# LeakyReLU on ScalarE out of PSUM, the mask from tanh in one pass, banks of their own, and a new order of all stages

## The reference

```
out  = conv3x3(x2, conv1) + b1
out  = (out - mean) * rsqrt(var + eps)          # per image and channel
out  = where(out >= 0, out, 0.2 * out)
out1 = conv3x3(out, conv2) + b2
mask = sigmoid(conv3x3(out, mask_w) + mask_b)
xm   = out * mask
q, k, v = 1x1 convolutions of xm (k and v of the padded xm)
attn = softmax over the 3x3 neighbours of sum_c q * k
out2 = sum over the neighbours of attn * v
y    = x2 + out1 * mask + (1 - mask) * out2
```

## Time and profile before

| | |
|---|---|
| median of 3 runs | 208.28 us (207.56 to 209.03) |
| the profiled execution | 207.95 us |
| its span, first to last instruction | 206.2 us |
| busy: PE, PEld | 177.2 us (86%), 117.6 us (57%) |
| busy: DVE, ACT, POOL | 153.4 us (74%), 106.3 us (52%), 71.2 us (35%) |
| granted TensorE clock, mean | 0.992 |

### The profile page before, as it was taken

The page is one execution under the profiler, slowest core; times in us unless marked ns, Lnnn a source line. Parts: engine busy times, 40 slices in busy tenths (PEclk is TensorE's granted clock), DMA queues, the critical chain, the costliest instruction groups (busy, mean ns, idle before and its releaser), DMA issues.

```text
span 206.2 us, 7265 instructions
## 1 busy us (share of the span) xinstructions
PE 177.2 (86%) x3161; PEld 117.6 (57%) x3161; DVE 153.4 (74%) x362; ACT 106.3 (52%) x192; POOL 71.2 (35%) x60
## 2 busy tenths in 40 slices
PE   1699989999867999999687999999688798999981
PEld 1557727748454555787347456876446344666841
DVE  6796499948697968697788993993838765992782
ACT  2173554313683732718982714449614774955650
POOL 8600530550005411750008640850404022670390
PEclk9999999999999999999999999999999789999999
DMA  6512014000230000001000040000100000000002
GB/s 190 104 57 60 0 26 121 10 10 6 76 103 29 0 15 10 3 6 41 0 3 0 0 122 5 6 3 13 56 3 5 0 3 10 5 8 5 6 0 105
DMA packets 11312, 6.34 MB, mean 31 GB/s; under 512 B 9168, under 2 KB 9648, under 8 KB 11280
## 3 DMA queue, kind: packets, MB, share of 16 engines
q1 hardware_dynamic: 11040, 5.29, 9.9%
q10 hardware_dynamic: 240, 0.58, 0.9%
HBM read 3.35 MB, written 1.05 MB: 21 GB/s over the span
## 4 chain that ended last, share of the span: by engine, by line
PE 56%; DVE 18%; ACT 9%; issue 6%; DMA 4%; SPq 3%; POOL 1%; DVEq 0%; ACTq 0%
PE ps L1473 9%; PE ps L1376 8%; PE ps L1435 7%; PE ps L1349 5%; PE ps L1342 5%; PE ps L1386 4%; PE ps L1536 3%; DVE sh_in L326 3%; DMA w3b<-in_w_gi 3%; PE ps L1508 2%; PE ps L1497 2%; SPq L395 2%; PE ps L1334 2%; PE ps L1519 2%; ACT p_t L733 2%
## 5 line engine op out<-in xcount | busy, mean ns | idle before, releaser
L483 POOL TENSOR_TENSOR ln_s<-ln_s,neg_half 128x16 f32<-128x16 f32 x7 | 20.5, 2929 | 63.3 <-DVE ln_s L940 63.3
L1435 PE MATMUL ps<-ln_out,w_gi 32*64 32x256 f32 x1152 | 33.7, 377 | 1.2 <-DVE x L1082 0.8
L1435 PEld LDWEIGHTS ps<-ln_out,w_gi 32*64 32x64 f32 x1152 | 25.6, 130 | 7.3 <-issue 2.4
L1376 PE MATMUL ps<-w_qk,sh_ln 128*128 128x128 f32 x192 | 23.2, 278 | 3.6 <-DMA sh_ln<-ln_out 2.4
L1473 PE MATMUL ps<-sh_in,w_in 96*32 96x256 f32 x384 | 23.8, 396 | 1.5 <-DVE sh_in L326 1.5
L1376 PEld LDWEIGHTS ps<-w_qk,sh_ln 128*128 128x128 f32 x192 | 22.1, 192 | 5.1 <-issue 4.0
L1342 PE MATMUL ps<-busy 128*128 128x512 bf16 x79 | 21.3, 407 | 0.0
L1473 PEld LDWEIGHTS ps<-sh_in,w_in 96*32 96x32 f32 x384 | 11.9, 114 | 12.5 <-issue 3.6
L618 ACT ACTIVATE sh_ln<-ln_out 32x512 f32<-32x512 f32 (+1 forms) x29 | 15.2, 524 | 5.2 <-DVE ln_out L918 4.8
L618 ACT ACTIVATE sh_x<-x 32x496 f32<-32x496 f32 (+1 forms) x20 | 12.3, 616 | 3.7 <-DVE x L1082 3.2
L618 ACT ACTIVATE sh_in<-act_c 32x496 f32<-32x496 f32 (+1 forms) x20 | 12.3, 617 | 3.2 <-DVE act_c L1140 2.9
(11 more groups left out here) (142 smaller groups left out, 333.1 us busy)
## 6 DMA issues: line engine op xcount, KB each, us to landing
x_res<-in_x SPq DMA_DIRECT2D x4, 256.0 KB, 2.9
out_x<-out_s SPq DMA_DIRECT2D x4, 256.0 KB, 2.5
sh_ln<-ln_out SPq DMA_DIRECT2D x15, 64.0 KB, 2.1
x_norm<-in_x SPq DMA_DIRECT2D x3, 256.0 KB, 3.0
kc<-in_shape_consts ACTq DMA_DIRECT2D x1, 450.0 KB, 5.0
w3b<-in_w_gi SPq DMA_DIRECT2D x1, 288.0 KB, 5.2
x_norm<-in_x SPq DMA_DIRECT2D x2, 128.0 KB, 2.8
ln_out<-ln_out SPq DMA_DIRECT2D x8, 25.5 KB, 2.4
```

What stands on the lines that cost most here:

```text
L483: nc.gpsimd.tensor_tensor(ln_s[n][:, 3, :], ln_s[n][:, 2, :], neg_half[:, :], ALU.pow)\
L1376: mm = nc.tensor.matmul(to, sh_ln1[pair % 2][:, d, i, WD * y:WD * y + P], w_qk[:, dy, :, :, :].rearrange("p d m c -> p (d m c)"), start=(d ...
L1435: mm = nc.tensor.matmul(ps[EC * i:EC * i + EC, r, BLK * m:BLK * m + BLK], w_gi[rows, dx, m, dy, :], src[rows, i, dy:dy + RH, dx:dx + W], s ...
```

## The change

- ScalarE computes LeakyReLU (Prelu, alpha 0.2) straight from conv1's PSUM bank, two images one after the other, with the negated mean (plus the conv's bias) as bias; `conv1_evac`, `center` and VectorE's `lrelu` go. One more small VectorE operation makes that bias, `I_NEG`.
- `scaled_act` also halves, and `masked` is (th + 1) * act_in, per image; msk goes. 1 - msk is made by VectorE from th, behind `masked`. The halo and `window_q` wait for `masked` alone.
- Of the planes "in", the block s = 1, r = 0 goes to DMA on SP, ScalarE's s = 1 block to VectorE; VectorE still has seven. The planes ln1 of pair 3 are shared out as those of pair 2.
- Head scores, attention output and r1 get banks of their own; `qk` then waits for the gated product of the pair in front, not for x2. The x1 sum is a stage of its own.
- The order of the stages on all engines is new. Six gate rounds stand behind `window_q` and `window_k`, where fillers stood; half of image 1's qk comes before conv1; on VectorE `ln1_apply` of pair 3 stands before the window probabilities. Fillers: 17 in the head's front become 6, and 9 in each step go.
- Banks 4 and 7 are cleared at the start by VectorE; POOL's constant of ones goes.

The diff, cut, first the signals and banks:

```diff
+        planes_by["in"]["dma"] = signal("in_planes_dma", 16, start=1)
         def head_bank(pair):
-            return 6 if pair == 1 else 3
+            return (3, 5, 7, 7)[pair]
+        def attn_bank(pair):
+            return (3, 5, 4, 4)[pair]
+        def reduce_banks(pair):
+            return (0, 1) if pair == PAIRS - 1 else (6, 7)
```

On SP's queue:

```diff
+            def in_planes(pair):
+                sp.wait_ge(g_lr.sem, g_lr.done(pair))
+                sp.wait_ge(g_c2.sem, g_c2.before(pair))
+                sp.dma_start(plane(sh_in)[C:2 * C, :, 1:1 + RH, :],
+                             act_c[0:C, :, :].rearrange("p i (y x) -> p i y x", x=W))\
+                  .then_inc(planes_by["in"]["dma"].sem, 16)
             def step(pair, norm):
-                if norm:
-                    load_norm(pair + 3)
                 load_res(pair + 2)
+                in_planes(pair)
                 ln2_edges(pair + 1)
                 halo(pair)
...
+            load_norm(2)
             ln1_planes(1)
-            load_norm(2)
             load_res(1)
+            load_norm(3)
```

On POOL:

```diff
             def step(pair, norm):
-                complement(pair)
-                residual(pair)
                 if norm:
                     rstd(0, pair + 3)
+                    residual(pair)
                     rstd(1, pair + 2)
...
```

On ScalarE:

```diff
-            def conv1_evac(pair, early=False):
...
+            def lrelu(pair, early=False):
+                act.wait_ge(g_in.sem, g_in.at(pair, 5))
+                act.wait_ge(g_sc.sem, g_sc.before(pair))
+                for e in ("dve", "dma"):
+                    act.wait_ge(planes_by["in"][e].sem, planes_by["in"][e].before(pair))
+                for i in range(2):
+                    ins = nc.scalar.activation(act_c[:, i, :], ps[:, conv1_bank(early), BLK * i:BLK * i + BLK], ACT.Prelu,
+                                               bias=inorm_v[:, I_NEG, i:i + 1], alpha=SLOPE)
+                ins.then_inc(g_lr.sem, 1)
             def step(pair, norm):
                 load_exp_table()
+                qk_t_evac(pair + 2, 0)
                 squares(1, pair + 1)
-                conv1_evac(pair)
-                qk_t_evac(pair + 2, 0)
+                lrelu(pair)
                 qk_t_evac(pair + 2, 1)
...
+                x2_planes(pair + 1)
                 pv_evac(pair)
-                x2_planes(pair + 1)
...
             key_windows(last)
             probs_t(but_last)
+            window_exp(last)
             out1_evac(last, True)
-            window_exp(last)
```

On VectorE:

```diff
+            for bank in (4, 7):
+                nc.vector.memset(ps[:, bank, :], 0.0).then_inc(s_zero_bd, 1)
...
             def masked(pair):
                 dve.wait_ge(g_th.sem, g_th.done(pair))
-                nc.vector.tensor_scalar(msk[:, :], th[:, :], 0.5, 0.5, ALU.mult, ALU.add).then_inc(g_xm.sem, 1)
...
+                for i in range(2):
+                    ins = nc.vector.scalar_tensor_tensor(
+                        out=xm[:, i, 1:1 + RH, 1:1 + W],
+                        in0=th[:, BLK * i:BLK * i + BLK].rearrange("p (y x) -> p y x", x=W), scalar=1.0,
+                        in1=act_in[:, i, :].rearrange("p (y x) -> p y x", x=W), op0=ALU.add, op1=ALU.mult)
+                ins.then_inc(g_xm.sem, 1)
+            def complement(pair):
...
+                nc.vector.tensor_scalar(omm[pair % 2][:, :], th[:, :], -0.5, 0.5, ALU.mult, ALU.add).then_inc(g_xm.sem, 1)
             def step(pair, norm):
+                if norm:
+                    x1_sum(pair + 1)
                 ln2_center(pair + 1)
+                inorm(pair)
                 ln_var(1, pair + 1)
-                inorm(pair)
                 inorm_mean(pair)
-                center(pair)
                 variance(pair)
-                lrelu(pair)
                 in_planes(pair)
+                ln2_apply(pair + 1)
                 head_scores(pair + 2)
-                ln2_apply(pair + 1)
                 scaled_act(pair)
                 head_max(pair + 2)
                 masked(pair)
+                complement(pair)
                 head_mix(pair + 2)
                 if norm:
                     ln1_center(pair + 3)
+                x1_sum(pair + 2)
+                if norm:
+                    ln_var(0, pair + 3)
                 else:
                     ln2_center(pair + 2)
                 window_softmax(pair)
-                ln_var(*((0, pair + 3) if norm else (1, pair + 2)))
-                window_probs(pair)
                 if norm:
                     ln1_apply(pair + 3)
                 else:
+                    ln_var(1, pair + 2)
+                window_probs(pair)
+                if not norm:
                     ln2_apply(pair + 2)
                 gated(pair + 1)
                 x2_all(pair + 1)
...
             ln1_center(2)
-            dve.wait_ge(s_wgi, 3)
-            clear(ps[:, 4, :], ps[:, 7, :])
+            ln_var(0, 2)
             ln2_apply(0)
             head_scores(1)
-            ln_var(0, 2)
+            ln1_apply(2)
             head_max(1)
             head_mix(1)
```

On TensorE:

```diff
             def qk(pair, i, halves=(0, 1)):
...
-                if not is_first(pair):
-                    pe.wait_ge(g_x2.sem, g_x2.before(pair - 1))
+                if pair > 1:
+                    pe.wait_ge(g_gi.sem, g_gi.at(pair - 2, 1))
             def step(pair, norm):
-                if not is_first(pair):
-                    attn_out(pair + 1)
                 qk(pair + 2, 0)
+                qk(pair + 2, 1, (0,))
                 conv1(pair)
+                qk(pair + 2, 1, (1,))
                 average_mean(pair)
-                qk(pair + 2, 1, (0,))
+                v_by_head(pair + 2, (0,))
                 average_var(pair)
-                qk(pair + 2, 1, (1,))
+                v_by_head(pair + 2, (1, 2))
                 gram(pair + 2)
-                v_by_head(pair + 2)
-                mask_conv(pair)
+                mask_conv(pair, images=(0,))
                 by_head(pair + 2)
+                mask_conv(pair, images=(1,))
+                front_read(pair + 2)
                 conv2(pair)
-                front_read(pair + 2)
-                stay_busy(2 if norm else 5, 5)
                 window_q(pair)
-                window_k(pair, busy_for=4)
-                if norm:
-                    stay_busy(3, 2)
-                else:
-                    attn_out(pair + 2)
+                gate_info(pair + 1, range(3))
+                window_k(pair)
+                gate_info(pair + 1, range(3, 6))
+                pe.wait_ge(g_q_sb.sem, g_q_sb.done(pair))
+                attn_out(pair + 2)
                 window_scores(pair)
+                pe.wait_ge(g_x1.sem, g_x1.done(pair + 2))
                 window_v(pair)
-                pe.wait_ge(g_x1.sem, g_x1.done(pair + 1 if norm else pair + 2))
-                gate_info(pair + 1, range(12))
+                gate_info(pair + 1, range(6, 15))
                 probs_transposed(pair)
-                gate_info(pair + 1, range(12, 18))
+                gate_info(pair + 1, range(15, 18))
                 window_out(pair)
...
             pe.wait_ge(s_busy, 1)
-            stay_busy(12, 5)
-            pe.wait_ge(g_im[0].sem, g_im[0].done(0))
-            stay_busy(5, 5)
+            stay_busy(4, 5)
             pe.wait_ge(s_wready, W_QKV)
             qk(0, 0)
+            stay_busy(2, 5)
             qk(0, 1)
...
-            pe.wait_ge(g_x2.sem, g_x2.done(but_last))
+            pe.wait_ge(g_gi.sem, g_gi.done(but_last))
             gate_info(last, range(6))
```

More of the change, by code:

```diff
@@ L206, in build @@
                      "dma": [(0, 2), (0, 3), (1, 0), (1, 1)]}
-        copies[2] = {"dve": [(3, r) for r in range(R)], "act": [(2, r) for r in range(R)],
-                     "dma": [(s, r) for s in (0, 1) for r in range(R)]}
+        for n in (2, 3):
+            copies[n] = {"dve": [(3, r) for r in range(R)], "act": [(2, r) for r in range(R)],
+                         "dma": [(s, r) for s in (0, 1) for r in range(R)]}
         g_xn = signal("x_for_norm_loaded", 16)
@@ L457, in _ @@
             but_last, last = PAIRS - 2, PAIRS - 1
+            in_planes(but_last)
             halo(but_last)
+            in_planes(last)
             halo(last)
@@ L591, in _ @@
             residual(but_last)
-            complement(last)
             residual(last)
@@ L762, in step @@
                 q_evac(pair)
+                if norm:
+                    squares(0, pair + 3)
                 k_evac(pair)
@@ L816, in _ @@
             out1_evac(but_last)
-            conv1_evac(last, True)
             q_evac(but_last)
+            lrelu(last, True)
             k_evac(but_last)
@@ L1112, in inorm_mean @@
                 dve.wait_ge(g.sem, g.at(pair, 4))
+                nc.vector.scalar_tensor_tensor(out=inorm_v[:, I_NEG, :], in0=inorm_v[:, I_MEAN, :], scalar=-1.0,
+                                               in1=vec[:, V_BC1:V_BC1 + 1].broadcast_to([P, 2]),
```

(23 more changed lines are left out.)

117 lines of the change are left out of this document (40 added, 77 removed).

## The result

The changed kernel takes 215.57 us (median of 4 runs, 212.52 to 217.13) against 207.92 us of the kernel before in the same comparison. The ratio, 1.0225 with a 95% interval of 1.0143 to 1.0308, leaves out the two runs of 216.77 and 217.13 us, which ran in a slower state (mean granted clock 0.932); the other two, 214.38 and 212.52 us (0.949 and 0.953), have a mean of 213.45. The changed kernel is slower than the one before; whether by more than 2% the interval leaves open. The forecast was 198.3 us, and the range ended at 204.5. The profiled execution took 214.38 us (span 212.6, mean granted clock 0.949; before 0.992).

The account below looks back on a forecast made before the run. TensorE was taken as busiest, with the chain's waits read for where it does not set the time. Gains of 2.9 + 0.7 + 2.9 + 1.75 + 1.4 = 9.65 from 207.95 gave 198.3 us; range 192.5 to 204.5.

Parts of the forecast that it names:

- the in-plane copy "to SP and DMA, hidden": First tail part: one shifted copy goes to SP and DMA, hidden; uncovered it would cost under 1 us.
- step 1: Second stretch between conv1 starts: 44.27 to 41.35 us, -2.9, from -4.1 to -1.2.
- the marks of being wrong: Granted clock near 0.5 in a step, more table loads, or TensorE waiting on x1, halo or in-plane DMA.
- The clock rival: Fillers go, TensorE slows at waits, up to 1.7 us a fall; two falls 201.7, eight 211.9; chance 0.13.
- Step 0: First stretch between conv1 starts: 44.59 to 43.85 us, -0.7; -2.4 without contention, up to +3.1.
- the large wait: Step 0: TensorE's transposes wait 3.4 us for window probabilities behind ln1's apply on VectorE, contention of 1.7 included.
- The head: Run up to the first conv1: 61.16 to 58.25 us, -2.9, between -1.2 and -3.6.
- The first tail part: Between the last two conv1 starts: 18.86 to 17.1 us, -1.75, from -0.5 to -2.7.
- the table rival: Prelu needs its own table: eight extra loads of 1.283 us; 208.6, or 203.4 half hidden; chance 0.07.
- The second tail part: From the last conv1 to the last VectorE add: 34.76 to 33.4 us, -1.4, from 0 to -2.2.

Follow-up runs that it names:

- e1: The changed kernel with the store of pair 0 issued on SP's queue behind the in-plane copy, edges and halo of pair 1; 209.29 us, ratio 1.0006.
- e7: e5 plus filler matmuls ahead of the mask convolution of both steps, the head maxima and the transposes of step 0; 202.77 us, ratio 0.971.
- e5: e1 plus VectorE doing the head scores ahead of LayerNorm 2's apply; 203.41 us, ratio 0.9745.
- e11: e12 plus probabilities before LayerNorm 1's apply, gate GELU before page copies, two page copies to VectorE, five fillers, earlier head maxima, own last-sum buffer; 197.07 us.
- e12: e5 with POOL's residual of pair 0 ahead of the power for LayerNorm 1 of pair 3; 201.71 us, ratio 0.9619.
- e2: The changed kernel with 34 filler matmuls ahead of the mask convolution of step 1; 210.13 us, ratio 1.0036.
- e3: The changed kernel with step 0's window probabilities ahead of LayerNorm 1's apply on VectorE, their copies ahead of page copies on ScalarE; 216.02 us, ratio 1.0223.
- e10: The changed kernel with only the head scores ahead of LayerNorm 2's apply on VectorE; 213.83 us, ratio 1.0198.

## Why the prediction was wrong

**The step that failed: the in-plane copy "to SP and DMA, hidden".** The prediction priced the transfer and asked what stands behind it on SP's queue (edges and halo). It did not ask what it stands behind: in step 1, the store of pair 0, which waits for POOL's `final`, and that stands behind the powers and the scaled weights. This place of `final` and of the store is the one that they had before; new is the copy behind the store. Nor did the prediction cost the copy in the steps at all; it priced it in the tail, where the store ahead of it goes out at 162.85, before LeakyReLU is done at 165.45. Two of the marks of being wrong that the prediction listed came true: a stretch of a step with a granted clock near 0.5, and, without a price, TensorE waiting on the in-plane DMA.

Of the 11.6 us of step 1, the waits from conv1 to r1 are 5.7 (9.6 counted against 3.9 forecast), the clock is 4.7, and the work 1.3, as in step 0; from r1 to conv1 it took 4.8, as summed. Of the 9.6 us 7.53 are the wait for the copy. With that gone (e1), waits of 0.98 and 2.65 stand in its place, where the prediction had 1.7: it did not charge the stretching of LayerNorm 2's apply beside `final`.

The Trainium skill, page "DMA: Bandwidth & Descriptors", section "Anatomy of one DMA — SWDGE (gpsimd) path", says that a semaphore wait is served on the issuing sequencer, ahead of the dispatch, and that DMA engines wait for none. It fits SP here: of TensorE's 7.53 us 4.70 passed before SP issued the copy, and the transfer itself took 2.59.

**The clock rival was right in kind and wrongly priced.** It charged 1.7 us a fall by the earlier trace rows, and gave a slower kernel 0.06. The fall behind the 7.5 us wait cost 4.7, since 24 and 72 half-speed matmuls stand behind it; the one behind the 4.89 us wait of step 0 slowed 1.6 us of work, and filling that wait gave back 0.6 (e7). Removing the fillers was not the loss, the waits were: the fillers that went from the steps had stood behind conv2, not at these waits; step 1 of e5 keeps its clock without them; and with the waits mended (e11) the granted clock is 0.996 with five fillers more than the change left.

**Step 0: three terms too small.** Work between the waits was 38.9 us against 37.45 summed (+1.4), the waits 7.6 against 6.4 (+1.2), the clock 1.6 against nothing. Of the work, 0.6 is the second half of the transposes (four matmuls, 0.63 at the upper level in step 1), which the sum leaves out: the chain ends with the first half. At 3.5 us over before, the stage lies past the prediction's own upper end of 3.1. The mechanism of the large wait was as described, VectorE's order plus its stretching beside POOL. The stretching was 3.0 us in three instructions against 1.7 charged, inside its bounds of 0 and 3.8; the wait 4.89 against 3.4. The Trainium skill, page "SBUF — State Buffer", section "SBUF: two separate sides", says that VectorE and GpSimd share one pair of ports under an exclusive lock, and that VectorE takes it when both its inputs are in SBUF (against a GpSimd operation that reads SBUF) or in a two-port mode. This case agrees: L951, L971 and even the small copy L982 (1.17 us) stretch, and the softmax out of PSUM at 0.64 to 0.66 beside the same residual doesn't (e12).

**What held.** The head (58.48 against 58.25): the four fillers, the queries beginning at 14.46, no wait for a DMA ahead of pair 2. In other kernels with the same head it ended between 57.2 and 59.1, so the last tenths are chance. The first tail part gained 2.2 us against 1.75 forecast, but not in the parts that the sum had: the mask convolution begins 10.05 us after conv1 instead of 10.69, so 0.6 sooner and not 1.0, and no fall of the clock is left there, which gives back 1.4 and not 0.75 (from the mask convolution to the next conv1 6.62 us instead of 8.00). That the sum came near is luck. LeakyReLU out of PSUM cost what the bounds said: 0.84 us the two passes, with 0.85 taken, it ended 1.3 us after the mean (1.5 forecast), and the table loads stayed seven in the whole execution, so the table rival is out.

```profile
164.42 0.16 DVE L1116 SCALAR_TENSOR_TENSOR inorm_v<-inorm_v,vec 128x2 f32<-128x2 f32 x1
...
164.61 0.84 ACT L678 ACTIVATE act_c<-ps,inorm_v 128x256 f32<-128x256 f32 x2 [4.50 <-DVE inorm_v L1116]
```

**The second tail part** gained 0.8 against 1.4. Moving the exponentials ahead of out1's copy was booked as part of the gain; VectorE's last sum then waited 2.34 us for POOL, for a buffer that both use. e11, with a buffer of its own, has 33.33: the 0.6 that were missing.

**Where the forecast gain lies.** e11 stands 1.2 us under the forecast of 198.3, with step 0 shorter and step 1 longer than the sum had them. So a gain of this size lies in these stages, but that does not make the sum right: it took corrections of the order on SP, VectorE, ScalarE and POOL, another split of the page copies, five fillers and a buffer, which the change does not have.

**What stays open.** Two waits of 0.98 and 0.47 us, some 2 us apart in step 0, were followed by a fall of the clock in the profiled executions of e2 and e3 (72 matmuls in 7.28 and 7.41 us) and not in those of the changed kernel and e1 (4.09). TensorE's program up to there is the same in all four. What decides it no run here shows. It may be part of the spread of 212.5 to 217.1 us: e3's execution, with such a fall, had a mean granted clock of 0.933. Nor was POOL's `final` moved ahead of the powers, which would take it from under LayerNorm 2's apply and free the store as well; what that gives is not known.

## What to carry to other kernels

Before a copy is moved to a DMA queue, write down what stands ahead of it on that queue and what each of these waits for; the transfer's own time says little. A wait that is removed uncovers the next: mend in the order of the chain and measure after each, since the second correction alone gave nothing that could be told from the spread, and 5.9 us behind the first. Put GpSimd's element-wise work under VectorE work that reads PSUM: here that took 1.6 us from one wait (e12).

## What the runs showed of the hardware

- VectorE's small copy of 128 x 112 took 1.17 us beside a GpSimd subtraction (changed kernel) and 0.22 without it (e12), and GpSimd's own operations on 128 x 512 went from 1.27 to 1.72 and 2.04 us: both sides lose.
- The same 72 matmuls take 4.09 us at the upper clock level and 6.67 to 7.41 us with the lower one in most of their run (e10, e3). The fall can cost more than the waits before it: 3.3 us behind waits of 0.98 and 0.47 (e3).
- ScalarE's Prelu with a bias per partition takes 0.84 us for two passes of 256 elements out of PSUM, behind a load of the Exp table (at 111.76 in the changed kernel) as behind one of the GELU table (at 164.61), and needed no load beyond the seven of the kernel before.
